# Re-sequencing two transposes, a state update and GpSimd's work in a chunked gated-linear-attention + MoE kernel

## The reference, cut to what matters

```
h = layernorm(x) * (1 + ca) + sa
q, k, v = h @ Wq, h @ Wk, h @ Wv                    # 16 heads of 16
g = log_sigmoid(h @ Wgk1 @ Wgk2 + bgk2) / 16
state = state * exp(g_t) + v_t k_t^T ; o_t = state q_t     # over all tokens in order
x1 = x + ga * ((layernorm(o) * gamma + beta) * silu(h @ Wg)) @ Wout
h2 = layernorm(x1) * (1 + cb) + sb
top-2 of 8 experts by h2 @ Wr + br, softmax over the two
out = x1 + gb * sum_e weight_e * (gelu(h2 @ W1_e + b1_e) @ W2_e + b2_e)
```

## Time and profile before

| | |
|---|---|
| median of 3 runs | 1105.98 us |
| the profiled execution's own time | 1107.52 us |
| its span | 1105.7 us |
| TensorE busy | 942.5 us (85%), mean granted clock 0.933 |
| VectorE busy | 737.2 us (67%) |
| ScalarE busy | 483.7 us (44%) |
| GpSimd busy | 426.0 us (39%) |
| DMA | 62.68 MB, mean 57 GB/s |

### The profile page before, as it was taken

How to read it: one execution, slowest core, us unless ns; L and a number is a source line. 1 busy time by engine, 2 the same in 40 slices (tenths; PEclk the granted TensorE clock), 3 DMA queues, 4 the chain that set the end, 5 groups by cost and what they waited for, 6 DMA issues and landing times.

```text
span 1105.7 us, 27202 instructions
## 1 busy us (share of the span) xinstructions
PE 942.5 (85%) x7313; PEld 760.0 (69%) x7314; DVE 737.2 (67%) x1909; ACT 483.7 (44%) x1548; POOL 426.0 (39%) x452
## 2 busy tenths in 40 slices
PE   5888878888788788887862999999999999999995
PEld 4455445555455554554532998999898999989995
DVE  2476777777777777778764666666666666666663
ACT  1555455454454554545420444434344444434441
POOL 4344443544435435444331232333332333323233
PEclk9899898898898988989965999999999999999998
DMA  7911110110111101111014622222122222212221
GB/s 241 328 30 46 39 39 34 39 49 34 39 35 43 44 34 41 42 38 39 30 36 133 202 46 35 39 35 42 31 43 34 39 39 37 42 33 40 34 42 22
DMA packets 51451, 62.68 MB, mean 57 GB/s; under 512 B 6273, under 2 KB 46930, under 8 KB 51282
## 3 DMA queue, kind: packets, MB, share of 16 engines
q1 hardware_dynamic: 38546, 44.36, 12.5%
q0 software_dynamic: 12864, 17.83, 9.4%
HBM read 38.91 MB, written 23.27 MB: 56 GB/s over the span
## 4 chain that ended last, share of the span: by engine, by line
PE 58%; DVE 12%; issue 12%; ACT 8%; DVEq 6%; SPq 3%; DMA 2%; POOL 0%; POOLq 0%; ACTq 0%
PE p_a L1084 22%; PE p_qk L1084 10%; PE p_vg L1084 8%; PE p_z L1084 8%; PE p_cum L1084 5%; SPq L444 2%; PE p_tr L1084 2%; DVE st L790 1%; ACT w L727 1%; ACT w L725 1%; PE p_o L1103 1%; DVE w L899 1%; PE p_tr L1265 1%; ACT host_o L720 1%; DVE host_s L940 1%
## 5 line engine op out<-in xcount | busy, mean ns | idle before, releaser
L641 POOL DMA_INDIRECT out_dram<-x,tok x68 | 163.5, 2404 | 345.5 <-DVE x L1061 322.7
L661 ACT ACTIVATE h2T<-p_tr,mods 128x128 f32<-128x128 f32 x200 | 80.3, 452 | 291.6 <-PE p_tr L1265 244.0
L1084 PE MATMUL p_a<-w_hi_r,host_s_r 128*128 x544 | 146.1, 300 | 12.1 <-DVE host_s_r L1068 12.1
L1084 PE MATMUL p_a<-w_r,host_s_r 128*128 x544 | 140.5, 290 | 0.0
L1084 PE MATMUL p_a<-w,qkT_both 64*128 64x512 f32 x256 | 92.3, 804 | 35.4 <-DVE host_s L940 30.1
L1038 DVE COPY host_x<-w 128x1024 f32 x68 | 47.3, 696 | 97.4 <-issue 51.9
L1084 PEld LDWEIGHTS p_a<-w_hi_r,host_s_r 128*128 128x128 f32 x544 | 102.0, 188 | 14.5 <-issue 14.2
L589 POOL TENSOR_TENSOR ln_host<-w,gam 128x256 f32<-128x256 f32 x32 | 23.1, 723 | 226.2 <-DVE w L899 226.2
L1084 PEld LDWEIGHTS p_a<-w_r,host_s_r 128*128 128x128 f32 x544 | 102.2, 188 | 0.2
L621 POOL DMA_INDIRECT expert_rows<-rows,pos x64 | 66.9, 1045 | 76.9 <-DVE pos L968 67.1
L845 DVE TENSOR_TENSOR w_hi<-p_a,upto 128x512 f32<-128x512 f32 x128 | 84.7, 683 | 2.1 <-PE p_a L1084 1.7
(11 more groups left out here) (206 smaller groups left out, 2173.2 us busy)
## 6 DMA issues: line engine op xcount, KB each, us to landing
w<-in_L_ffn_W_dram SPq DMA_DIRECT2D x16, 1024.0 KB, 12.6
ln_host<-expert_rows SPq DMA_DIRECT2D x68, 136.0 KB
host_x<-in_L_attn_x_dram SPq DMA_DIRECT2D x64, 128.0 KB, 2.1
out_dram<-x SPq DMA_DIRECT2D x32, 128.0 KB, 1.8
w<-in_L_wmod_dram SPq DMA_DIRECT2D x1, 1536.0 KB, 6.8
expert_rows<-pad_rows SPq DMA_DIRECT2D x8, 136.0 KB, 1.8
out_dram<-x,tok POOLq DMA_INDIRECT x68, 4.7
b_all<-in_L_ffn_b_dram SPq DMA_DIRECT2D x1, 1024.0 KB, 8.1
```

The source lines that it names most:

```text
L641: nc.gpsimd.indirect_dma_start(out=out, out_offset=bass.IndirectOffsetOnAxis(ap=tok[u][:, 0:1], axis=0), in_=y_out[u][:], in_offset=None, ...
L661: last = A.activation(dst[:, j, :], src[:, j * P:(j + 1) * P], ACT.Identity, scale=mods[:, which + 2 + j:which + 3 + j], bias=mods[:, whic ...
L1084: return nc.tensor.matmul(dst, lhsT, rhs, start=start, stop=stop, skip_group_check=True)
```

## The change

Several instructions of a step get another place on their engine. Nothing is computed differently.

- **TensorE.** The transposes x2T and ot move from the end of a step to the next step, behind the first scores (x2T is then of chunk s - 2, ot of chunk s - 1). The update u goes into `p_z`, columns 0 to 255, in place of `p_a[0]`; the wait for `u_taken` moves from ahead of the scores to ahead of the gate's rank product. u comes after the routing's rank products. The second block's scores come behind the transposes of the normalised output and of q, k. The first block's output goes ahead of the cumulative sums, the second behind them.
- **VectorE.** `o_tok` and its statistics move to the next step, behind the first two masks, interleaved with the statistics of x. silu's last product goes behind x1. The routing weights (L932 to L934) go ahead of `vn`. In the tail, the picks and sums follow without `o_tok` between them.
- **ScalarE.** The inverse root of the attention output's variance goes behind h2T and the copy rT. `gap_e` goes behind the z chain. `modulate_x` goes ahead of the inverse root for x1 and of the exponentials.
- **GpSimd.** `qbd` goes ahead of the two scales.

```diff
@@ GpSimd step
-                    pool.wait_ge(silu_ready, f + 1)
-                    after(pool, o_ln_ready, f - 1)
-                    nc.gpsimd.tensor_tensor(w_ln[v][:], silu[:], gam[:], ALU.mult)
-                    nc.gpsimd.tensor_tensor(b_ln[v][:], silu[:], bet[:], ALU.mult).then_inc(ln_scales_ready, 1)
-
                     pool.wait_ge(qkT_taken, f + 1)
...
                     last.then_inc(qbd_ready, 1)
+
+                    pool.wait_ge(silu_ready, f + 1)
+                    after(pool, o_ln_ready, f - 1)
+                    nc.gpsimd.tensor_tensor(w_ln[v][:], silu[:], gam[:], ALU.mult)
+                    nc.gpsimd.tensor_tensor(b_ln[v][:], silu[:], bet[:], ALU.mult).then_inc(ln_scales_ready, 1)
@@ ScalarE step
-                if finish:
-                    inverse_root(mv_o, s - 1, o_stats, o_scale)
                 if route:
                     act_e.wait_ge(x2T_ready, s - 1)
...
                     A.copy(rT[0:RANK, :], p_z[0:RANK, D:D + P]).then_inc(rT_ready, 1)
+                if finish:
+                    inverse_root(mv_o, s - 1, o_stats, o_scale)
+                if front:
                     act_e.wait_ge(projqk_ready, f + 1)
...
-                if route:
-                    act_e.wait_ge(gap_ready, s - 1)
-                    A.activation(gap_e[:], gap[:], ACT.Exp).then_inc(gap_exp, 1)
...
                     A.activation(lz[:], ez[:], ACT.Ln, bias=1.0).then_inc(log1p_ready, 1)
-
+                if route:
+                    act_e.wait_ge(gap_ready, s - 1)
+                    A.activation(gap_e[:], gap[:], ACT.Exp).then_inc(gap_exp, 1)
+                if front:
...
+                if nextx:
+                    modulate_x(s + 2)
                 if finish:
                     inverse_root(mv_1, s - 1, x1_stats, x1_scale)
...
-                if nextx:
-                    modulate_x(s + 2)
@@ VectorE step
-                bo.begin(s)
+                bo.begin(d)
...
                 if finish:
+
+                    dve.wait_ge(ot_ready, d + 1)
+                    bo.mark(V.tensor_tensor(o_tok[:], p_o[:, D:2 * D], e_pos[v][:], ALU.mult))
+                if nextx:
+                    ln.begin(s + 2)
+                    x_loaded(s + 2, u)
+                    ln.mark(V.bn_stats(st_x[:], x_in[u][:]))
+                if finish:
+                    bo.sync()
+                    bo.mark(V.bn_stats(st_o[:], o_tok[:]))
+                if nextx:
+                    ln.sync(apart=True)
+                    V.bn_aggr(mv_x[:, 0:2], st_x[:]).then_inc(x_stats, 1)
+                if finish:
+                    bo.sync(apart=True)
+                    V.bn_aggr(mv_o[:, 0:2], st_o[:]).then_inc(o_stats, 1)
...
-                if nextx:
-                    norm_x(s + 2, u)
...
-                if front:
-                    dve.wait_ge(sigmoid_ready, f + 1)
-                    V.tensor_tensor(silu[:], p_vg[:, D:2 * D], silu[:], ALU.mult).then_inc(silu_ready, 1)
                 if finish:
...
                     V.tensor_tensor(x1[v][:], p_o[:, D:2 * D], x_res[v][:], ALU.add).then_inc(x1_ready, 1)
+                if front:
+                    dve.wait_ge(sigmoid_ready, f + 1)
+                    V.tensor_tensor(silu[:], p_vg[:, D:2 * D], silu[:], ALU.mult).then_inc(silu_ready, 1)
+                if finish:
                     dve.wait_ge(x1_ready, d + 1)
-                    statistics(yo, x1[v][:], st_1, mv_1, x1_stats)
+                    yo.mark(V.bn_stats(st_1[:], x1[v][:]))
...
+                if finish:
+                    yo.sync(apart=True)
+                    V.bn_aggr(mv_1[:, 0:2], st_1[:]).then_inc(x1_stats, 1)
                 if route:
+                    ro.sync()
+                    ro.mark(V.tensor_tensor(wt[:, 2:3], gap_e[:], wt[:, 1:2], ALU.mult))
+                    ro.then(V.tensor_scalar(wt_a[:], hot[0][:], wt[:, 1:2], None, ALU.mult))
+                    V.scalar_tensor_tensor(out=rows[u][:, D:D + E], in0=hot[1][:], scalar=wt[:, 2:3],
+                                           in1=wt_a[:], op0=ALU.mult, op1=ALU.add)
+                if front:
...
                     standardise(rows[v][:, 0:D], x1[v][:], mv_1, d, x1_scale).then_inc(xn2_ready, 1)
-                if route:
-                    ro.sync()
-                    ro.mark(V.tensor_tensor(wt[:, 2:3], gap_e[:], wt[:, 1:2], ALU.mult))
-                    ro.then(V.tensor_scalar(wt_a[:], hot[0][:], wt[:, 1:2], None, ALU.mult))
-                    V.scalar_tensor_tensor(out=rows[u][:, D:D + E], in0=hot[1][:], scalar=wt[:, 2:3],
-                                           in1=wt_a[:], op0=ALU.mult, op1=ALU.add)
                 if back:
                     dve.wait_ge(u_ready, s + 1)
                     after(dve, state_ready, s)
-                    V.tensor_tensor(state_sum[:], p_a[0][:, 0:D], state[:], ALU.add).then_inc(u_taken, 1)
+                    V.tensor_tensor(state_sum[:], p_z[:, 0:D], state[:], ALU.add).then_inc(u_taken, 1)
...
-                if back:
-
-                    dve.wait_ge(ot_ready, s + 1)
-                    bo.mark(V.tensor_tensor(o_tok[:], p_o[:, D:2 * D], e_pos[u][:], ALU.mult))
...
-                if back:
-                    bo.sync()
-                    bo.mark(V.bn_stats(st_o[:], o_tok[:]))
...
-                if back:
-                    bo.sync(apart=True)
-                    V.bn_aggr(mv_o[:, 0:2], st_o[:]).then_inc(o_stats, 1)
@@ TensorE step
                     if j == 0:
-                        after(pe, u_taken, s)
                         after(pe, am_ready, 4 * s)
...
                 if front:
                     pe.wait_ge(hT_ready, f + 1)
+                if route:
+                    pe.wait_ge(xn2_ready, s - 1)
+                    after(pe, score_taken, s - 2)
+                    transposes(p_tr[:, D:2 * D], rows[u], KD, x2T_ready)
+                if finish:
+                    pe.wait_ge(oT_taken, s)
+                    transposes(p_o[:, D:2 * D], oT, KD, ot_ready)
+                if front:
                     after(pe, g_ready, f)
                 if front or route:
                     after(pe, ranks_taken, s - 2)
+                if front or finish:
+                    after(pe, u_taken, s)
...
-                if back:
-                    scores_of_block(1)
...
                     transposes(p_qk, qk[v], 2 * KD, qkT_ready)
+                if back:
+                    scores_of_block(1)
...
                     transpose_x(s + 2, u, s - 1)
+                if back:
+                    after(pe, x1_ready, s)
+                    after(pe, state_ready, s)
+                    pe.wait_ge(vn_ready, s + 1)
+                    output_of_block(0)
                 if front:
                     pe.wait_ge(g_ready, f + 1)
...
                     last.then_inc(cum_ready, 1)
                 if back:
-                    after(pe, x1_ready, s)
-                    after(pe, state_ready, s)
-                    pe.wait_ge(vn_ready, s + 1)
-                    output_of_block(0)
                     output_of_block(1).then_inc(o_ready, 1)
-
-                    for j in range(KD):
-                        last = mm(p_a[0][:, j * P:(j + 1) * P], qk[u][:, D + j * P:D + (j + 1) * P],
-                                  vn[u][:, j * HB:(j + 1) * HB, :], True, True)
-                    last.then_inc(u_ready, 1)
-                if finish:
-                    if nextx:
-                        pe.wait_ge(hT_ready, s + 3)
-                    if route:
-                        pe.wait_ge(score_taken, s - 1)
-                    pe.wait_ge(xn2_ready, s)
-                    transposes(p_tr[:, D:2 * D], rows[v], KD, x2T_ready)
                 if route:
                     pe.wait_ge(chosen_ready, s - 1)
                     mm(p_z[:, RANKS:RANKS + E], before_b[:], chosen[:], True, True)
                     mm(p_z[:, RANKS + E:RANKS + 2 * E], ones_b[:], chosen[:], True, True).then_inc(rank_ready, 1)
                 if back:
-                    pe.wait_ge(oT_taken, s + 1)
-                    transposes(p_o[:, D:2 * D], oT, KD, ot_ready)
+
+                    for j in range(KD):
+                        last = mm(p_z[:, j * P:(j + 1) * P], qk[u][:, D + j * P:D + (j + 1) * P],
+                                  vn[u][:, j * HB:(j + 1) * HB, :], True, True)
+                    last.then_inc(u_ready, 1)
```

More of the change, by code:

```diff
@@ L786, in _ @@
             ln, bo, oo, yo, ro = (Order(dve, s) for s in (dve_ln, dve_b, dve_o, dve_y, dve_r))
-            def statistics(o, src, st, mv, stats):
-                o.then(V.bn_stats(st[:], src), apart=True)
-                V.bn_aggr(mv[:, 0:2], st[:]).then_inc(stats, 1)
             def standardise(dst, src, mv, n, scale):
@@ L796, in standardise, with x_loaded @@
                 return V.tensor_scalar(dst, src, mv[:, 0:1], mv[:, 2:3], ALU.subtract, ALU.mult)
-            def norm_x(n, u):
-                ln.begin(n)
+            def x_loaded(n, u):
                 if isinstance(n, int):
```

(23 more changed lines are left out.)

1 line of the change is left out of this document (removed).

## The result

The changed kernel takes 1010.8 us (median of 4 runs, 1009.1 to 1012.2) against 1106.3 for the one before (1105.9 to 1108.5): a ratio of 0.913, 95% interval 0.912 to 0.915. Faster, as forecast, but by more than the range allowed for: 1035 was predicted, with 1016 as its low end.

The account below looks back on a forecast made before the run. The prediction took a ring of waits, with no engine full, plus TensorE's falling clock as the bound. 29 x (17.05 - 14.6) = 71 us off 1107.5 gave 1036.5, less 1.5 for the median: 1035 us, range 1016 to 1071.

Parts of the forecast that it names:

- The clock: TensorE's granted clock in the 29 steps, mean 0.91, was to stay full, giving back 1.23 us a step.
- Rival 1: Ring shorter, but TensorE's clock still falling as now: 1071 us, chance 0.17.
- the rule: TensorE's clock falls only when idle time fills a whole look of the chip; closing the scores' gap could then return nothing: 1071 us.
- The walk up to the state sum: One step at full clock, followed engine by engine from VectorE's first instruction: state sum at 12.3 us, against 13.5 before.
- Weights ahead of vn: VectorE's three routing operations, moved into its wait for the exponentials, end at 11.8 if held by GpSimd, 10.4 if not.
- the tail: VectorE from state sum to next step: 2.30 becomes 1.7 us, up to 2.4 if GpSimd holds picks; branch adds 0.2.
- Start and drain: The stretches before and after the 29 steps were put at zero change, give or take 2 us.
- 2 (ring as long): Rival: TensorE's clock full, but the ring of waits as long as now: 1070 us, chance 0.12.
- 3: Rival: ring as long and clock still falling, so no change: 1106 us, chance 0.04.
- 4 (slower by ScalarE's root pair): Rival: root pair for o blocks ScalarE ahead of the qk copy, TensorE runs dry, clock falls: 1134 us, chance 0.09.

Follow-up runs that it names:

- b_bank: Kernel before, with the state update written to p_z, rank products ahead of it and the first scores no longer waiting for u_taken: 1073.9 us, ratio 0.970.
- f1: Changed kernel with x's statistics moved in step s = 1, cumulative sums ahead of block 0, and one routing weight computed as 1 - w: 992.3 us.
- a_tail_delay: Changed kernel with two tiny VectorE operations, results unused, put ahead of the picks: 1030.0 us, ratio 0.931.
- a_weights_back: Changed kernel with VectorE's three routing weight operations put back behind the standardised row: 1047.8 us, ratio 0.947.
- a_start: Changed kernel with x's statistics put behind the layer norm of o, only in step s = 1: 1008.7 us, ratio 0.912.
- a_wait: Changed kernel with the first scores waiting for u_taken, the state sum, again: 1036.5 us, ratio 0.937.

## Why the prediction was right in direction and wrong in size

**The clock: right.** It is at 1.00 through the 29 steps, and b_bank shows that taking the scores' wait away is enough for that. Rival 1 fell, and with it the rule as the prediction put it after the Trainium skill ("TensorE: Matmul & The Clock Gate", "Why this matters for your kernels"). The page's row warns of long idle times between groups of matmuls; the "only" is the prediction's own word, and it is the "only" that the traces refute: no idle time of TensorE in the 29 steps is longer than 1.25 us, the clock stood at 0.50 for 6.8 us all the same, and it was full once one of the two such waits was gone. By that rule b_bank had no clock to give back; it gained 32.7 us, and since its step (15.88) is as long as the fast one of before (15.82), that gain is clock.

**The walk up to the state sum: right.** Measured against predicted, t = 0 at 300.56: statistics of o at 2.9 (2.9), output copy 5.8 (6.1), z chain 7.0 (7.3), x1 8.4 (8.7), sums 10.3 (10.5), exponentials 11.3 (11.5), state sum at 12.2 (12.3). The idle time before block 0 was to be 1.2 us and is 0.92.

**Weights ahead of vn: right, including their bound.** I took them as held by GpSimd, ending at 11.8; they end at 11.4 (311.99 less 300.56), a hair behind the exponentials (11.3). By the Trainium skill ("GPSIMD Engine Reference", "Key points") VectorE contends with GpSimd in instructions with two SBUF inputs and in those of a 2-port performance mode. The rows agree on the first: L934, with two inputs, takes 0.71 us on average, and 0.15 in f1 with one. L935, with one tensor input and a scalar taken from SBUF, is held just as well (0.78), and so is the cast L971; whether they ran in such a mode no row here shows.

**The step that failed: the tail.** "Without `o_tok` and bn_stats between (0.68 us), 2.30 becomes 1.7. One or two picks may still be held ..." I took 2.1 and 0.2 for the loop's branch: 2.3. Measured from state sum to L848 are 1.48 and 1.65 in turn (299.08 to 300.56, 312.78 to 314.43), branch included, 1.57 on average: 0.73 x 29 = 21 us of the 24.2 that separate forecast and median. The 2.30 from before still contained a held pick, 0.70 us instead of the 0.16 of the drain. I used that row as an upper bound on new holds and left the old one standing in the lower one. Without it the tail is 2.30 - 0.68 - 0.54 = 1.1, which would have given a step of 13.4 to 13.6 and a time below the range; measured were 13.77. Most of what lies between 1.1 and the measured 1.48 is the cast L971, which the walk had at its short value: 0.43 instead of 0.15 us, in every one of the 29 steps. So one hold went (0.54 us) and a smaller one came (0.28). What released the pick is GpSimd's own time. Before, its second state product waited for the state sum, started 0.56 us behind it and took the second pick with it, as the timeline of the kernel before shows beside L949 (336.08):
```profile
336.04 0.72 POOL L613 TENSOR_TENSOR host_s<-host_s,w 128x256 f32<-128x256 f32 x1 [0.50 <-DVE host_s L940]
```
Now L610 runs from 299.09, so L613 starts only 0.82 us behind the state sum, when both picks are done, and it is the cast that it takes with it. That this is a matter of place is shown twice. In a_tail_delay two constants in front bring the hold of a pick back, and 0.63 us a step. In a_weights_back L610 is over before the state sum, L613 starts 0.56 us behind it, and the second pick is held as in the kernel before.

**Start and drain, put at zero.** They are +2.6 and -3.5 us; that they nearly cancel is luck. The start's part is x's load in front of o's statistics, which a_start takes out (2.2 us). I had moved `o_tok` past that load in VectorE's queue without asking what the load does in the start. Where in the drain the 3.5 us came from was not tried; a_start, whose code is the same there, has 546.5 us behind the last mark where the changed kernel has 545.3, so a part of it may be scatter.

What is left of the difference is 0.1 us a step in the walk (2.9 us) and this 0.9. That makes 25.0 with the 21 of the tail, against 24.2, because the forecast took the median 1.5 us below the profiled execution, and for the changed kernel it lies 0.6 below (1010.8 against 1011.4).

**Rivals.** 2 (ring as long) and 3 fell with the marks. 4 (slower by ScalarE's root pair) fell: L671 starts right behind its operand, at 303.48, and the qk copy ends at 3.9.

## What to carry to other kernels

When a ring of waits is walked, ask of each duration taken from it whether it holds a wait for another engine, and take its value on the unloaded engine as one end of the range: a hold lasts until the running GpSimd instruction ends, here up to 0.7 us, and a tenth of a microsecond decides whether there is one. Price a removed wait twice, in ring time and in clock; b_bank and a_wait show the same wait paid in one currency and then in the other. And try the parts of a change singly: of the two transposes moved here one cost 0.7 us a step when undone and the other nothing, while the dearest to undo (1.3 us) were three tiny instructions that merely changed place, 0.34 us of it in a hold elsewhere that their move had released.

## What the runs showed of the hardware that I had not expected

- Small VectorE instructions beside a running GpSimd `tensor_tensor` end 0.02 to 0.04 us after it, whatever they need by themselves: two-input `tensor_tensor` of one element a partition 0.71 us, `tensor_scalar` with an SBUF scalar 0.78, the cast of two elements 0.43 or 0.15, the pick 0.69 or 0.15. A larger one, L848 in f1 (128x256), ended 0.28 us after it. A `tensor_scalar` with constants (0.15, or 0.22 in a_tail_delay), statistics and instructions that read PSUM weren't stretched in these timelines.
- Behind two waits of TensorE of 1.15 and 1.25 us near each other the clock fell to 0.50; so it did in 19 of the 29 steps (mean 0.82 or 0.90) and not in the other 10, though the waits are the same; with one of 1.20 us and one of at most 0.9 us behind the scores, in b_bank, it stood at 0.99 over the whole stretch.
- Putting three moves back together (+0.50 us a step) cost less than one of them alone (+0.91).
